# A DLRM tower on one core: blocks of 256, 512, 512, 512 and 256 samples, and one-hots of 513 columns

## What is computed

```python
combined = concatenate([dense_features[:, None, :], e], axis=1)      # 2048 x 27 x 128
interactions = einsum('bfd,bgd->bfg', combined, combined)            # upper triangle: 351 per sample
h = concatenate([dense_features, interactions_flat, dense_features], axis=1)   # 607
h = maximum(h @ W_top1 + b_top1, 0.0)                                # 512
h = maximum(h @ W_top2 + b_top2, 0.0)                                # 256
y = h @ W_top3                                                       # 1
```

## Time and profile before

| what | us |
|---|---|
| median of 3 runs | 428.83 (428.31 to 429.2) |
| the profiled execution | 430.39 |
| its span in the trace | 428.6 |
| TensorE busy | 379.9 (89%) |
| VectorE busy | 224.4 (52%) |
| ScalarE busy | 145.6 (34%) |
| GpSimd busy | 258.4 (60%) |

### The profile page before, as it was taken

The page is one execution under the profiler, slowest core; times in us unless marked ns, Lnnn a source line. Parts: engine busy times, 40 slices in busy tenths (PEclk is TensorE's granted clock), DMA queues, the critical chain, the costliest instruction groups (busy, mean ns, idle before and its releaser), DMA issues.

```text
span 428.6 us, 7915 instructions
## 1 busy us (share of the span) xinstructions
PE 379.9 (89%) x3308; PEld 274.0 (64%) x3308; DVE 224.4 (52%) x414; ACT 145.6 (34%) x320; POOL 258.4 (60%) x248
## 2 busy tenths in 40 slices
PE   7738976359999979988999979989999979989997
PEld 7626855248566648878566648878466558879442
DVE  2927995005843539805944439806935349707300
ACT  2432743211322234442322234443222334442321
POOL 6888888760477777760477777760577777750000
PEclk9986989859999999999999999999999999999999
DMA  5992222210022132420122132320122232210000
GB/s 199 388 319 74 61 76 55 68 51 10 26 65 71 49 81 62 104 69 9 28 68 66 53 84 59 103 69 9 34 73 61 55 76 74 68 44 5 2 0 0
DMA packets 19872, 30.74 MB, mean 72 GB/s; under 512 B 5657, under 2 KB 13977, under 8 KB 19836
## 3 DMA queue, kind: packets, MB, share of 16 engines
q0 software_dynamic: 7680, 15.74, 14.3%
q1 hardware_dynamic: 12148, 14.48, 10.9%
q10 hardware_dynamic: 8, 0.01, 0.0%
HBM read 30.21 MB, written 0.01 MB: 70 GB/s over the span
## 4 chain that ended last, share of the span: by engine, by line
PE 67%; POOL 21%; issue 6%; DMA 3%; ACT 2%; POOLq 0%
POOL rows L340 21%; PE mix_ps L420 16%; PE emb_ps L363 11%; PE emb_ps L364 11%; PE mix_ps L393 8%; PE emb_ps L393 7%; PE mix_ps L431 6%; PE emb_ps L374 4%; DMA rows<-table,gather_ids 3%; PE mix_ps L439 2%; PE emb_ps L405 1%; ACT h L508 1%; ACT emb L469 1%; DMA gather_ids<-ids_gathered 0%; ACT emb L459 0%
## 5 line engine op out<-in xcount | busy, mean ns | idle before, releaser
L340 POOL DMA_INDIRECT rows<-table,gather_ids x240 | 257.4, 1073 | 123.3 <-issue 70.1
L536 DVE TENSOR_SCALAR hot<-lids,row_number 128x512 fp32r<-128x512 int16 x352 | 160.3, 504 | 91.1 <-PE emb_ps L364 80.4
L363 PE MATMUL emb_ps<-hot,table_hl 128*128 128x512 f32 x352 | 153.0, 435 | 10.6 <-DVE hot L536 10.6
L364 PE MATMUL emb_ps<-hot,table_hl 128*128 128x512 f32 x352 | 139.3, 396 | 0.0
L363 PEld LDWEIGHTS emb_ps<-hot,table_hl 128*128 128x128 f32 x352 | 67.4, 191 | 30.3 <-issue 14.6
L469 ACT ACTIVATE emb<-emb_ps 128x512 f32<-128x512 f32 x64 | 43.6, 687 | 109.6 <-PE emb_ps L374 108.4
L364 PEld LDWEIGHTS emb_ps<-hot,table_hl 128*128 128x128 f32 x352 | 67.4, 191 | 18.7 <-issue 6.3
L459 ACT ACTIVATE emb<-emb_ps 128x512 f32<-128x512 f32 x44 | 50.2, 1141 | 80.5 <-PE emb_ps L364 80.5
L374 PE MATMUL emb_ps<-ident,rows 128*128 128x128 f32 x256 | 40.6, 285 | 22.2 <-DMA rows<-table,gather_ids 22.2
L546 DVE STREAM_TRANSPOSE turned<-mix_ps 32x832 uint32<-32x832 uint32 (+1 forms) x24 | 25.2, 1049 | 63.8 <-PE mix_ps L393 63.4
L374 PEld LDWEIGHTS emb_ps<-ident,rows 128*128 128x128 f32 x256 | 31.7, 146 | 34.9 <-DMA rows<-table,gather_ids 25.5
(11 more groups left out here) (27 smaller groups left out, 106.6 us busy)
## 6 DMA issues: line engine op xcount, KB each, us to landing
lids<-ids_looked_up SPq DMA_DIRECT2D x44, 128.0 KB, 3.1
raw<-table SPq DMA_DIRECT2D x11, 512.0 KB, 10.2
rows<-table,gather_ids POOLq DMA_INDIRECT x240, 2.7
rows<-dense SPq DMA_DIRECT2D x16, 64.0 KB, 1.8
w_sb<-w_pairs SPq DMA_DIRECT2D x2, 256.0 KB
w_sb<-w SPq DMA_DIRECT2D x1, 512.0 KB
w_sb<-w_dense SPq DMA_DIRECT2D x1, 256.0 KB
w_stage<-w_dense SPq DMA_DIRECT2D x1, 256.0 KB
```

The lines of the kernel that those rows point to most:

```text
L340: pool.indirect_dma_start(out=rows[:, use % ROW_SLOTS, q, :], out_offset=None, in_=tables[GATHERED[g]], in_offset=bass.IndirectOffsetOnAxi ...
L363: pe.matmul(bank[:, :], table_hl[:, i, 0, cols], hot[:, n % HOTS, :], start=(c == 0), stop=False)
L364: pe.matmul(bank[:, :], table_hl[:, i, 1, cols], hot[:, n % HOTS, :], start=False, stop=(c == CHUNKS - 1)).then_inc(hot_used, 1)
L536: dve.tensor_scalar(hot[:, n % HOTS, :], lids[:, k % LIDS, :], row_number[:, c:c + 1], None, ALU.is_equal).then_inc(hot_ready, 1)
```

## The change

The blocks become 2, 4, 4, 4 and 2 tiles (`BLOCK_TILES`). In the two blocks of 256 samples nine tables are looked up and 17 gathered, in groups of 3, 4, 3, 4 and 4 with the dense row; in the others it stays at 11 and 15. All matmuls and copies of a 256-sample block are as narrow.

The one-hots of the later blocks are written 513 (258 in the last block) columns wide, from ids that lie in three parts of 171 (86) with a gap behind each; the matmuls read the first 512 (256). The first block's ids come in one transfer (`first_lids`), its one-hots have 256 columns. The ring of one-hots shrinks from 10 to 8, the row slots from 8 to 7. GpSimd waits for all grams of the block before, as it did.

With the last group of a tile ACT also copies the dense features into `dense_x`, and layer 1 reads them there. The weights' loads stand behind the first dense rows on SP, the planned times are new, and layer 3 stands 9 us later in the plan.

```diff
-BLOCK_LOOKUPS = [11] * 4
+
+BLOCK_TILES = [2, 4, 4, 4, 2]
+BLOCK_LOOKUPS = [9, 11, 11, 11, 9]
...
-BLOCK = 512
+BLOCK = 128 * max(BLOCK_TILES)
...
-    ROW_SLOTS = 8
+    ROW_SLOTS = 7
...
-    HOTS = 10
+    HOTS = 8
     LIDS = 3
+
+    PARTS = 3
+    PADDED = [wide if b == 0 else -(-wide // PARTS) * PARTS for b, wide in enumerate(WIDE)]
+    LID_AT = [sum(PADDED[:b]) for b in range(BLOCKS + 1)]
...
+    LENGTH = [2.9 + 5.5 * 4 * n + 3.7 * n for n in BLOCK_TILES[:1]]
+    for b in range(1, BLOCKS):
+        LENGTH.append(5.1 * BLOCK_TILES[b - 1] + (0.93 * BLOCK_LOOKUPS[b] + 5.7) * BLOCK_TILES[b])
...
+    WEIGHTS_AT = 24.0
+    L3_LATER, EARLY = 9.0, 12.0
...
-    at(-5, "weights_load")
+    at(-18.5, "first_lids")
+    at(WEIGHTS_AT, "weights_load")
...
+        at(after + 8.0 + 17.5 * part, "h2", b)
+        at(after + 8.0 + 17.5 * part + L3_LATER, "l3", b)
...
-        hot = sb("hot", [128, HOTS, BLOCK], fp32r)
-        lids = sb("lids", [128, LIDS, BLOCK], i16)
+        hot = sb("hot", [128, HOTS, max(PADDED) + 1], fp32r)
+        PART_WIDE = -(-BLOCK // PARTS) + 1
+        lids = sb("lids", [128, LIDS, PARTS, PART_WIDE], i16)
+        dense_x = sb("dense_x", [128, BLOCK])
...
-        dense_part = bass.AP(emb, FEATURES - 1, [[EMB_WIDE, 128], [32 * PAIR_WIDE, BLOCK // 64], [SECOND, 2], [PAIR_WIDE, 32]])
...
+            def load_first_lids():
+
+                sp.dma_start(first_lids[:, :, :], bass.AP(ids_looked_up.tensor, 0, [[0, 128], [ids_looked_up.shape[1], BLOCK_LOOKUPS[0]], [1, WIDE[0]]])) \
+                    .then_inc(first_lids_in, 16)
...
-                sp.dma_start(lids[:, k % LIDS, :],
-                             ids_looked_up[i:i + 1, b * BLOCK:(b + 1) * BLOCK].to_broadcast([128, BLOCK])) \
+                sp.dma_start(lids[:, k % LIDS, :, 0:PADDED[b] // PARTS],
+                             ids_looked_up[i:i + 1, LID_AT[b]:LID_AT[b + 1]].to_broadcast([128, PADDED[b]])) \
...
-                if t % IN_BLOCK == 0:
+                if PLACE[t] == 0:
...
-                    x = dense_part
+                    x = dense_x[:, 0:WIDE[b]]
...
-                    wait(act, dense_used, t // IN_BLOCK)
-                at_pair = t % IN_BLOCK * 64 * PAIR_WIDE
+                    wait(act, dense_used, BLOCK_OF[t])
+                    act.activation(by_turn(dense_x[:, PLACE[t] * TILE:PLACE[t] * TILE + TILE]),
+                                   by_number(bank[:, 128 * n - 128:128 * n]), ACT.Copy)
...
+                wide = PADDED[b]
+                ids = first_lids[:, i, :] if b == 0 else lids[:, k % LIDS, :, 0:wide // PARTS]
...
-                    dve.tensor_scalar(hot[:, n % HOTS, :], lids[:, k % LIDS, :],
+                    dve.tensor_scalar(hot[:, n % HOTS, 0:wide], ids,
...
+    ends = np.cumsum(BLOCK_TILES) * 128
+    low_ids = np.concatenate([low_ids[:, :ends[0]]] + [np.pad(low_ids[:, a:b], ((0, 0), (0, -(b - a) % 3)), constant_values=-1)
+                                                       for a, b in zip(ends[:-1], ends[1:])], axis=1)
```

More of the change, by code:

```diff
@@ L53, in dlrm_tower @@
     TILES = BATCH // TILE
-    BLOCKS = BATCH // BLOCK
-    IN_BLOCK = BLOCK // TILE
+    BLOCKS = len(BLOCK_TILES)
+    FIRST_TILE = [sum(BLOCK_TILES[:b]) for b in range(BLOCKS + 1)]
+    BLOCK_OF = [b for b in range(BLOCKS) for _ in range(BLOCK_TILES[b])]
+    PLACE = [t - FIRST_TILE[BLOCK_OF[t]] for t in range(TILES)]
+    WIDE = [TILE * n for n in BLOCK_TILES]
+    assert len(BLOCK_OF) == TILES and all(n % 2 == 0 for n in BLOCK_TILES)
+    SECOND, PAIR_WIDE = 32, 59
+    EMB_AT = [(BLOCK - wide) // 2 * PAIR_WIDE for wide in WIDE]
     def grouped(features):
@@ L121, in dlrm_tower @@
     for b in range(BLOCKS):
[L122 to L135, removed]
+        rows_at, first = last_rows(b), FIRST_TILE[b]
+        for j in range(BLOCK_TILES[b]):
+            t = first + j
+            at(rows_at - 3.0 if j == 0 else rows_at + 0.5 + 3.6 * (j - 1), "gram", t)
+            at(rows_at + 0.4 if j == 0 else rows_at + 0.5 + 3.6 * j + 0.1, "turn", t)
+            at(rows_at + 0.5 + 3.6 * (j + 1) + 0.2, "pairs", t)
         after = ends(b)
@@ L138, in dlrm_tower @@
         for c in range(3):
-            at(after + 5.0 + 0.1 * c, "z", b, c)
-            at(after + 6.5 + 4.0 * c, "l1", b, c)
+            at(after + 5.5 + 0.1 * c, "z", b, c)
+            at(after + 6.5 + (0.5 + 0.9 * BLOCK_TILES[b]) * c, "l1", b, c)
+        part = BLOCK_TILES[b] / 4
         for n in range(N1):
[L142 to L146, removed]
+            at(after + 7.0 + (9.0 + 1.0 * n) * part, "h1", b, n)
+            at(after + 7.6 + (11.0 + 1.8 * n) * part, "l2", b, n)
+        at(after + 8.0 + 17.5 * part, "h2", b)
+        at(after + 8.0 + 17.5 * part + L3_LATER, "l3", b)
+    at(WEIGHTS_AT + 12.0, "weights")
     STEPS = [step for _, _, step in sorted(timed)]
@@ L315, in _ @@
             sp.dma_start(gather_ids[:, 0, :], ids_gathered[:, 0, :]).then_inc(first_ids_in, 16)
-            run({"load": load, "lids": load_lids, "drow": drow, "weights_load": weights_load})
+            run({"load": load, "lids": load_lids, "first_lids": load_first_lids, "drow": drow, "weights_load": weights_load})
         @block.gpsimd
@@ L352, in look @@
             def look(k, h):
-                use, i = ("look", k, 0), LOOKS[k][1]
-                bank = emb_bank(use)
+                use, (b, i) = ("look", k, 0), LOOKS[k]
+                bank = emb_bank(use, WIDE[b])
                 if h == 0:
@@ L362, in look @@
                     cols = slice(DIM * c, DIM * c + DIM)
-                    pe.matmul(bank[:, :], table_hl[:, i, 0, cols], hot[:, n % HOTS, :], start=(c == 0), stop=False)
-                    pe.matmul(bank[:, :], table_hl[:, i, 1, cols], hot[:, n % HOTS, :],
+                    pe.matmul(bank, table_hl[:, i, 0, cols], hot[:, n % HOTS, 0:WIDE[b]], start=(c == 0), stop=False)
+                    pe.matmul(bank, table_hl[:, i, 1, cols], hot[:, n % HOTS, 0:WIDE[b]],
                               start=False, stop=(c == CHUNKS - 1)).then_inc(hot_used, 1)
@@ L430, in l2 @@
                 for m in range(N2):
-                    last = pe.matmul(layer_bank(m), w2_sb[:, n, 128 * m:128 * m + 128], h1_x[:, n, :],
+                    last = pe.matmul(layer_bank(m, WIDE[b]), w2_sb[:, n, 128 * m:128 * m + 128], h1_x[:, n, 0:WIDE[b]],
                                      start=(n == 0), stop=(n == N1 - 1))
@@ L438, in l3 @@
                 for m in range(N2):
-                    last = pe.matmul(layer_bank(2)[0:1, :], w3_sb[:, m:m + 1], h2[:, m, :], start=(m == 0), stop=(m == N2 - 1))
+                    last = pe.matmul(layer_bank(2, WIDE[b])[0:1, :], w3_sb[:, m:m + 1], h2[:, m, 0:WIDE[b]], start=(m == 0), stop=(m == N2 - 1))
                 last.then_inc(l3_full, 1)
```

97 lines of the change are left out of this document (57 added, 40 removed).

## The result

| what | before | after |
|---|---|---|
| median, us | 429.01 (428.31 to 429.79, 4 runs) | 414.69 (413.28 to 416.59, 4 runs) |
| ratio, 95% interval | | 0.9664 [0.9629, 0.9699] |
| the profiled execution | 430.39 | 413.8 |
| its span | 428.6 | 412.0 |

A forecast was written before the change was run, and what follows sets the result against it. GpSimd's gathers and full stop were taken as the bound, TensorE a close second. Stops ending at 64.5, 155.7, 247.7 and 339.7, block 4 to 395.8, tail 17.9: 413.7; plus 1.8, less 1.6: 414 us, range 408 to 422.

The forecast's parts named there:

- The gathers of blocks 1 to 3: GpSimd's 60 gathers per middle block run unstretched at 0.94 us beside slow one-hots, 74.6 us instead of about 79.4.
- the gaps change nothing: Rival, 6%: one-hots stay at 0.39 us and gathers stay stretched, 427 us in all.
- the slow form contends as well: Rival, 5%: slow one-hots also stretch gathers, excess 8 to 13.5 us per middle block, 436 to 453 us.
- The one-hots: On VectorE, 513-column one-hots take 0.66 us each, up from 0.394, bounds 0.39 and 0.69; a block's 88 take 58 us.
- the ring decides: Rival, 10%: a one-hot takes 0.8 us, TensorE waits for VectorE, 6 us in blocks 2 and 3 each; 428 us.
- the tie: Blocks 2 and 3: TensorE, following VectorE's one-hots, starts the first gram 0.8 us late, at most 2 us.
- Block 0: First block: vector work stretches the 34 gathers by 9 us (0 to 11.5), so the last ends at 53.9.
- The stops: GpSimd's waits for a block's grams: 10.6 us behind the 2-tile block, 16.6 behind middle ones, including 0.3 for the dense copy.
- T + 74.6: T is the gram end from which TensorE's order was timed; 74.6 us later the last look is copied out.
- my walk: Step-by-step timing of TensorE's order from the gram end: layer 3 done at T + 48.3, last look copied at T + 74.6.
- the rival on short matmuls: Rival, 7%: 256-column matmuls in block 4 don't get shorter, 15 us more, 429 us.
- Block 4 and the tail: Last block: TensorE's work exceeds 42.4 us of gathers, last gram ends at T + 56.4, 395.8; tail behind it 17.9 us.

## Why the prediction was right, step by step

The sum held to 1.7 us for the profiled execution (412.0 of span against 413.7), because a term of −7 and three of about +2 cancel. That the total is this close is luck; the mechanism held, and the sizes did not. By the ends of the stops:

| stretch | predicted | measured | difference |
|---|---|---|---|
| to the first stop's end | 64.5 | 57.26 | −7.2 |
| block 1 | 91.2 | 92.8 | +1.6 |
| block 2 | 92.0 | 94.05 | +2.05 |
| block 3 | 92.0 | 93.8 | +1.8 |
| block 4 to its last gram's end | 56.1 | 56.0 | −0.1 |
| tail | 17.9 | 18.1 | +0.2 |

**The gathers of blocks 1 to 3: right.** 74.8 for the predicted 74.6. One row was misread on the way: at 112.97 VectorE was not idle but turned a gram out of `emb_ps`, from 111.49 to 114.68 in its timeline. That gathers beside an idle VectorE take 0.94 us holds by others (183.88 to 190.12, with VectorE idle to 193.82). The gather in the shadow of the slow form stays at 0.94 to 0.96, the end of the bounds that I took. The rivals "the gaps change nothing" and "the slow form contends as well" are out, the latter with a reason: 39.37 us of unbroken slow one-hots beside unstretched gathers.

**The one-hots: right.** 7.95 us for twelve, less the last one's 0.74 and over eleven, is 0.655 apart; 0.66 was predicted, and those of 258 columns start 0.39 apart for 0.40. The rival that the ring decides at 0.8 us is out. But the one-hots matter more than the tie allowed for, as below.

**Block 0: the mis-sized term.** I took 9 us of stretch (0 to 11.5); the 34 gathers run from 2.73 to 47.0 with three long ones, 1.65, 1.76 and 1.29 us. That is 2.2 us of stretch (44.3 − 42.1), and my bound of 0 was nearer: the 9 was 6.8 us too much. The step that failed carried the stretch per us of vector work over from one-hots of 512 columns to ones of 256. GpSimd's timeline of block 0 and VectorE's, in the changed kernel:

```profile
31.95 0.94 POOL L377 DMA_INDIRECT rows<-table,gather_ids  x1 [0.30 <-issue]
...
35.70 0.94 POOL L377 DMA_INDIRECT rows<-table,gather_ids  x1 [0.30 <-issue]
...
31.94 1.27 DVE L566 TENSOR_TENSOR table_hl<-raw,table_hl 128x1024 fp32r<-128x1024 f32 x1
33.13 2.64 DVE L580 TENSOR_SCALAR hot<-first_lids,row_number 128x256 fp32r<-128x256 int16 x8
35.69 1.27 DVE L566 TENSOR_TENSOR table_hl<-raw,table_hl 128x1024 fp32r<-128x1024 f32 x1
```

Three gathers and one look share a cycle of 3.75 us. Now it is VectorE that gives way: eight one-hots of 256 columns and a subtraction would take 8 × 0.26 + 1.14 = 3.2 us by my own figures, and take 3.75. The run with even one-hots, whose block 0 is the same, shows them alone, behind its last gather of the block, and there the cycle is 55.99 − 52.75 = 3.24. Its eight one-hots, and one of those beside the gathers in the changed kernel:

```profile
52.75 2.18 DVE L580 TENSOR_SCALAR hot<-first_lids,row_number 128x256 fp32r<-128x256 int16 x8
...
34.96 0.55 DVE L580 TENSOR_SCALAR hot<-first_lids,row_number 128x256 fp32r<-128x256 int16 x1
```

About every third one-hot takes 0.55 us where the rest take 0.34, and ends 0.1 us behind a gather (this one at 35.51, the gather at 35.40). The Trainium skill, "SBUF — State Buffer", section "Who interferes with whom", says that of a two-port vector instruction and a GpSimd one the first to issue blocks the other. The trace agrees with both sides of it: the gather of 2.86 us shows GpSimd waiting, this stretch VectorE. The long gathers of 1.65 and 1.76 us here each meet a subtraction that started before them. The other half of the step, that the ids may come late, came true: the first one-hot starts at 13.34 after 4.59 us of waiting for `first_lids`, and 9 × 3.75 us from there still ends by 48.

**The stops: 10.6 right by luck, 16.6 and 17.4 too short.** ACT's dense copy takes 0.41 us for my 0.3. The 10.6 came from the 17.73 of the earlier trace rows, and that stop had a slow gram in it, behind a wait for rows, in TensorE's timeline of the kernel before:

```profile
91.87 1.11 PE L374 MATMUL emb_ps<-ident,rows 128*128 128x128 f32 x4 [3.94 <-DMA rows<-table,gather_ids]
92.92 5.69 PE L393 MATMUL mix_ps<-emb 128*64 128x52 f32 x128
```

The first stop now, 10.25, has none; instead its first gram starts at 47.44, 0.4 us behind the end of the last gather, where the old one started 1.1 us ahead of it. The slow gram has moved to block 1: its 18.02 holds one of 5.73 us, at a granted clock of 0.50, behind TensorE's wait of 4.40. I had given block 1 "half the layers in front", so a TensorE that waits for rows, and no price for its clock, though the row at 92.92 was there to give it. The stop is 1.4 of the missing 1.6; the gathers are the other 0.2.

**The tie in blocks 2 and 3: the right mechanism, its size 2.8 instead of 0.8.** The first gram of block 2 should have started at T + 74.6 and does at 226.53, T + 76.8, behind the last look's copy and not behind rows. The chain in order of time (start, duration, what) has it:

```profile
222.71 0.41 PE emb_ps L400
...
223.35 0.42 PE emb_ps L400
...
224.01 0.42 PE emb_ps L400
...
225.36 1.13 ACT emb L496
...
226.53 3.94 PE mix_ps L430 x128
```

The looks' matmuls start 0.65 us apart, in step with the one-hots: VectorE and the ring of 8 set the end of the block, as the step said. They start late because layer 3 ends at T + 50.4 and not at T + 48.3. Of these 2.1 us, 0.3 are the first half look (first pair transpose at T + 6.7 for T + 6.4), about 1 is a wait that my walk had not: layer 2 stands before ACT's h_x, 2.9 us in three blocks, which is behind a copy into emb on ACT:

```profile
L468 PE MATMUL mix_ps<-h_x,w_sb 128*128 128x512 f32 x48 | 22.5, 598 | 2.9 <-ACT h_x L542 2.9
```

For the remaining 0.8 I have no row. Everything behind it is pushed back by the same 2.1. The dense layer's eight records take 3.70 us for the 3.45 predicted.

**Block 4 and the tail: right.** 56.0 for 56.1, the 256-column matmuls 0.12 apart (347.85, 347.97, 348.09), which ends the rival on short matmuls; and 18.1 for 17.9, TensorE's wait before z 2.74 for the 3 predicted, with no clock lost behind it. That is not assured, since the kernel without the stop lost 1.1 us behind the same wait; my "2 us at most" covered it. The two stretches by engine:

```profile
337.60:393.90 56.30, 54.71 (x500) 39.79 (x500) 35.05 (x78) 20.75 (x59) 32.15 (x34) 1.00 0.20 49
393.90:412.00 18.10, 12.83 (x62) 9.81 (x58) 3.15 (x3) 5.31 (x20) 0.00 (x0) 0.98 0.00 0
```

The median came out at 414.69 for 414; the 1.6 us that I took off the profiled execution's time by the kernel before was not to be had (here the median is 0.9 above it), and this hid most of the 1.7.

## What to carry to other kernels

Before pricing a stretched gather by VectorE's busy time, look at the form of the vector instruction beside it: a slower form of the same work can be free for the engine that waits for memory, if VectorE has room. When the engine that set the period is sped up, price the second one's walk to the same point to within a us: here its chain through ACT and the ring was 2 us longer than thought and took half of what the gathers gave back. And after such a change ask again what each full stop still buys; this one had become harmful in one block and idle in the others.

## What the runs showed of the hardware

- A gather under twelve fast one-hots of 512 columns takes 2.86 us for 0.94; beside one-hots of 256 columns, in the same fast form, most gathers stay at 0.94 and VectorE's cycle gets longer instead (3.75 us for 3.24). I had expected the same side to wait in both.
- TensorE's first gram behind a wait of 4.40 us takes 5.73 instead of 3.94 us, at a granted clock of 0.50. Behind a wait of 2.74 us in the tail the changed kernel, twice, shows no loss (layer 1 5.45 us, clock 1.00), and the kernel without the stop, behind the same 2.74, takes 6.15, its clock at 0.50 at first. The length of the wait alone does not settle it.
- A chip can be in a condition in which the same program, the kernel before, takes 85 to 95 us longer by the medians, with pauses at much the same places from run to run. Operations of GpSimd and VectorE are unchanged in it (gathers 0.94, one-hots of 513 columns 0.74); TensorE's clock is granted at 0.50 in the pauses, and a look's matmul takes 0.79 for 0.47. A comparison with the kernel before on the same chip does not repair this, since the pauses may weigh differently on each kernel: the dense copy alone looks 4% and 3% faster there, the gaps alone the same. What causes it stays open.
